# A three-layer block (attention, state-space, two routed feed-forwards): softplus as one ScalarE function, router maxima as an exponential's bias, the last residual sum on TensorE, and a new placement

## The reference

```
x = x + attention(LN(x))      # RMS norm, 16 heads of 16, causal; returns xn + out
x = x + ffn(LN(x))
x = x + ssm(LN(x))
x = x + ffn(LN(x))

ffn(x):  base = x W + b;  shared = low-rank of rank 16
         gate = softmax(x Wr + br) over 6 experts, the two largest kept and renormalised
         routed = sum over experts of weight * (x A_e) B_e, rank 16
ssm(x):  xc = silu(causal conv of 4 taps);  delta = softplus(xc Wd + bd);  B = xc Wb;  C = xc Wc
         h[t] = exp(A * delta[t]) * h[t-1] + delta[t] * xc[t] * B[t]     (256 features x 16 states)
         y[t] = sum over states of h[t] * C[t]
         return (y * sigmoid(x Wg + bg)) Wo + bo
```

## Time and profile before

| | us |
|---|---|
| median of 3 runs | 2177.48 (2174.78 to 2177.67) |
| the profiled execution, device time | 2174.6 |
| its span, first to last instruction | 2172.8 |

### The profile page before, as it was taken

One profiled execution on the slowest core, in us unless ns is written; L12 is line 12 of the kernel. 1 busy time (PEld: TensorE's weight loads), 2 busy tenths in 40 slices (PEclk: granted clock), 3 DMA queues, 4 the chain that ended last, 5 costly groups with the idle time before them and its releaser, 6 DMA issues.

```text
span 2172.8 us, 33597 instructions
## 1 busy us (share of the span) xinstructions
PE 1840.5 (85%) x11393; PEld 1129.0 (52%) x11424; DVE 1675.5 (77%) x2570; ACT 1407.8 (65%) x2724; POOL 1087.5 (50%) x946
## 2 busy tenths in 40 slices
PE   5779788988889898988989888998989898868765
PEld 3446454646556464646556464655556464535333
DVE  5343678889788888879787888879887888977673
ACT  2445767686676767686775867687775777664531
POOL 0000365555455464656465454656555564666672
PEclk8999999999999999999999999999999999989887
DMA  4312377666767576666767576667767577651110
GB/s 114 83 53 58 92 156 152 150 138 142 144 149 159 128 168 146 154 136 146 164 133 154 136 157 137 149 138 157 161 136 155 124 161 145 132 113 45 41 57 10
DMA packets 185916, 275.53 MB, mean 127 GB/s; under 512 B 33537, under 2 KB 125586, under 8 KB 185746
## 3 DMA queue, kind: packets, MB, share of 16 engines
q1 hardware_dynamic: 155506, 163.27, 30.4%
q0 software_dynamic: 30240, 110.11, 27.3%
HBM read 128.58 MB, written 34.08 MB: 75 GB/s over the span
## 4 chain that ended last, share of the span: by engine, by line
PE 42%; ACT 19%; DMA 16%; SPq 7%; issue 5%; DVE 5%; POOL 5%; POOLq 0%; ACTq 0%; DVEq 0%
PE bank L312 7%; DMA sk<-qk_parts 6%; PE bank L516 5%; SPq L712 5%; PE bank L321 4%; ACT dec L896 3%; PE bank L370 3%; PE bank L393 3%; ACT pt L781 3%; PE bank L418 3%; DMA out<-X 3%; PE bank L499 3%; DMA qk_parts<-parts 3%; PE bank L480 2%; DMA y<-hc 2%
## 5 line engine op out<-in xcount | busy, mean ns | idle before, releaser
L1133 DVE TENSOR_TENSOR_SCAN hc<-dec,inp 128x1024 f32<-128x1024 f32 x256 | 613.2, 2395 | 42.5 <-ACT dec L896 30.5
L1304 POOL TENSOR_TENSOR inp<-u,b_all 128x512 f32<-128x512 f32 x256 | 355.3, 1388 | 393.7 <-DVE hc L1133 140.1
L781 ACT ACTIVATE pt<-bank 128x512 f32<-128x512 f32 x640 | 373.8, 597 | 223.8 <-PE bank L395 221.0
L1306 POOL TENSOR_TENSOR inp<-u,b_all 128x512 f32<-128x512 f32 x256 | 375.6, 1467 | 20.1
L370 PE MATMUL bank<-sk,sq 96*128 96x512 bf16 (+3 forms) x1024 | 278.5, 311 | 100.8 <-DMA sk<-qk_parts 64.9
L896 ACT ACTIVATE dec<-dt,a_neg 128x511 f32<-128x511 f32 x512 | 338.0, 717 | 32.6 <-DVE hc L1133 32.6
L1140 DVE TENSOR_TENSOR hc<-hc,bank 128x1024 f32<-128x1024 f32 x242 | 293.9, 1214 | 56.2 <-PE bank L555 55.3
L1313 POOL DMA_DIRECT2D y<-hc x210 | 186.1, 886 | 245.5 <-DMA y<-hc 121.5
L393 PE MATMUL bank<-sq,sk 98*128 98x512 bf16 (+3 forms) x1024 | 274.7, 307 | 35.7 <-ACT pt L781 30.0
L1012 DVE TENSOR_REDUCE mall<-bank 128x1 f32<-128x512 f32 x256 | 172.7, 675 | 108.2 <-PE bank L372 108.0
L370 PEld LDWEIGHTS bank<-sk,sq 96*128 96x128 bf16 x1024 | 102.0, 100 | 219.5 <-DMA sk<-qk_parts 74.0
(11 more groups left out here) (165 smaller groups left out, 3509.9 us busy)
## 6 DMA issues: line engine op xcount, KB each, us to landing
y<-hc POOLq DMA_DIRECT2D x210, 512.0 KB, 5.5
b_all<-b_kept SPq DMA_DIRECT2D x256, 256.0 KB, 4.0
qk_parts<-parts SPq DMA_DIRECT2D x96, 256.0 KB, 2.5
sq<-qk_parts SPq DMA_DIRECT2D x384, 64.0 KB, 3.7
sk<-qk_parts SPq DMA_DIRECT2D x384, 64.0 KB, 3.9
X<-in_x SPq DMA_DIRECT2D x16, 512.0 KB, 6.2
out<-X SPq DMA_DIRECT2D x16, 512.0 KB, 5.8
sq<-hlt SPq DMA_DIRECT2D x256, 2.0 KB
```

The lines of the kernel that those rows point to most:

```text
L781: A(pt[:, n % PT, :], score_bank[unit % 2][:, :], ACT.Exp).then_inc(exp_done.sem, 1)
L1133: V.tensor_tensor_scan(h, d, v, 0.0, ALU.mult, ALU.add).then_inc(scan_done.sem, 1)
L1304: G.tensor_tensor(inp[:, n % 2, 0, :], u[:, 0, :], b_all[:, k % 3, :], ALU.mult).then_inc(pool_own.sem, 1)
L1306: G.tensor_tensor(inp[:, n % 2, 1, :], u[:, 1, :], b_all[:, k % 3, :], ALU.mult).then_inc(inp_ready.sem, 1)
```

## The change

- `dt` comes from ACT's own Softplus, straight from the projection's bank; Relu, Abs, Exp, Ln and DVE's sum are gone. `dt` now has two buffers, and the silu's Tanh is kept in one of them instead of in `sp_t`. Both halves are placed in slot 150 on ACT; on PE they stay in 149 and 152, and both stay in bank `MA`.
- The router's maximum is taken negated and used as the bias of the exponential, one ACT instruction for each of four token blocks; DVE's subtraction is gone.
- In the last feed-forward PE adds X itself, with one more matmul by the identity per token block, and ACT copies the bank to X (`finished`); DVE's `add_to_x` is gone.
- The tables are new. Besides shifts by one to five slots, `load_x` moves from slot -119 to -116, that is from just behind `store` to behind the last third of `stack`. In `BANK` change: res (0, 1) to (0, 0), xn (1, 0) to (0, 0), hw0 1 to 0, up0 (0, 1) to (1, 0), turn1 (0, 1) to (1, 0), up1 (1, 0) to (0, 1).

```diff
     FRAME = 2 * UN * NG
-    PE_AT = {"res": (-32, -31), "xn": (-75, -71), "qk00": (-52, -50, -48), "qk01": (-50, -47, -44), "v": (-26, -32),
-             "qk10": (-6, -4, -3), "qk11": (-4, -2, 0), "ao": (92, 92), "x1": (95, 97), "turn0": (105, 108),
-             "low0": 109, "hw0": 121, "up0": (124, 125), "xs": (135, 135), "conv": (137, 141), "gate": (146, 140),
-             "bc": (149, 152, 154), "dt": (149, 152), "x3": (251, 252), "turn1": (262, 265), "low1": 265, "hw1": 275,
-             "up1": (278, 279)}
...
-    ACT_AT = {"res": (-30, -28), "square_f": 98, "square_s": 127, "square_l": 252, "norm_q": -94, "norm_f": 103,
-              "exp0": 115, "norm_s": 131, "softplus": 153, "decays": 160, "norm_l": 257, "exp1": 266,
-              "xn": (-76, -71), "qk00": (-52, -50, -47), "qk01": (-50, -49, -44), "v": (-26, -32),
-              "qk10": (-6, -4, -1), "qk11": (-4, -2, 0), "ao": (91, 92), "turn0": (104, 108), "low0": 110,
-              "hw0": 120, "xs": (135, 138), "conv": (139, 141), "gate": (146, 140), "bc": (149, 152, 154),
-              "dt": (149, 152), "turn1": (263, 263), "low1": 264, "hw1": 275}
-    DVE_AT = {"add_x1": (94, 96), "in0": 113, "out0": 116, "add_up0": (123, 124), "silu": 144, "delta": 155,
-              "gated": 246, "add_x3": (251, 251), "in1": 265, "out1": 268, "add_up1": (277, 280), "stats_q": -102}
-    POOL_AT = {"rsqrt_f": 99, "rsqrt_s": 124, "rsqrt_q": -104, "inputs": 151, "rsqrt_l": 254, "low": (111, 266)}
-    SP_AT = {"parts": (-43, -4), "load_x": -119, "store_b": 155, "store": 281}
+    PE_AT = {"res": (-32, -30), "xn": (-77, -71), "qk00": (-52, -50, -47), "qk01": (-49, -47, -44), "v": (-26, -32),
+             "qk10": (-7, -4, -3), "qk11": (-4, -2, 0), "ao": (91, 92), "x1": (95, 99), "turn0": (105, 108),
+             "low0": 109, "hw0": 121, "up0": (123, 124), "xs": (135, 135), "conv": (137, 140), "gate": (146, 139),
+             "bc": (149, 152, 154), "dt": (149, 152), "x3": (251, 251), "turn1": (264, 265), "low1": 265, "hw1": 276,
+             "up1": (278, 278)}
...
+    ACT_AT = {"res": (-32, -30), "square_f": 98, "square_s": 124, "square_l": 252, "norm_q": -92, "norm_f": 103,
+              "exp0": 116, "norm_s": 132, "decays": 160, "norm_l": 256, "exp1": 264, "xn": (-78, -72),
+              "qk00": (-52, -50, -46), "qk01": (-49, -49, -44), "v": (-26, -32), "qk10": (-7, -4, -1),
+              "qk11": (-4, -2, 0), "ao": (91, 91), "turn0": (104, 108), "low0": 110, "hw0": 120, "xs": (135, 138),
+              "conv": (139, 140), "gate": (146, 139), "bc": (149, 152, 154), "dt": (150, 150), "turn1": (263, 263),
+              "low1": 264, "hw1": 276, "up1": (278, 279)}
+    DVE_AT = {"add_x1": (94, 96), "in0": 114, "out0": 116, "add_up0": (123, 124), "silu": 143, "delta": 152,
+              "gated": 246, "add_x3": (251, 251), "in1": 265, "out1": 268, "stats_q": -106}
+    POOL_AT = {"rsqrt_f": 98, "rsqrt_s": 121, "rsqrt_q": -103, "inputs": 154, "rsqrt_l": 251, "low": (111, 266)}
+    SP_AT = {"parts": (-42, -4), "load_x": -116, "store_b": 152, "store": 281}
     FINISH = 14
...
                     pe.wait_ge(side["hw", f].free, side["hw", f].at("hw", b, f))
+                if f:
+                    pe.wait_ge(side["x3", j].free, side["x3", j].at("x3", b, j))
                 pe.wait_ge(m.free, m.fill(("up", b, f, j)))
...
                         mm(dst, xt[:, c, tb * P:(tb + 1) * P], wbase[:, c, :], start=(c == 0), stop=False)
+                    if f:
+                        mm(dst, ident[:, :], X[:, b % XS, tb, :], start=False, stop=False)
                     last = mm(dst, hwt[:, tb * P:(tb + 1) * P], wup[:, :], start=False, stop=True)
...
             def exp_logits(b, f):
-                act.wait_ge(lg_done[f].sem, lg_done[f].at(b))
-                A(ex[:, :, :], lg[:, :, :], ACT.Exp).then_inc(ex_done[f].sem, 1)
+                act.wait_ge(top_done[f].sem, top_done[f].at(b))
+                for tb in range(TB):
+                    last = A(ex[:, tb, :], low[:, f, tb, LR - E:], ACT.Exp, bias=top[:, f, tb:tb + 1])
+                last.then_inc(ex_done[f].sem, 1)
...
+            def finished(l, j):
+
+                m = side["up", 1, j]
+                act.wait_ge(m.full, m.at("up", l, 1, j))
+                copy(X[:, l % XS, 2 * j:2 * j + 2, :], m.tile[:, :].rearrange("p (t d) -> p t d", t=2)).then_inc(m.free, 1)
+
             def sigmoid_gate(f, c):
...
                 m = side["conv", c]
+                act.wait_ge(u_done.sem, u_done.at(f - 1))
+                act.wait_ge(dec_ready.sem, dec_ready.at(f - 2))
                 act.wait_ge(m.full, m.at("conv", f, c))
-                A(sp_t[:, c, :], m.tile[:, :], ACT.Tanh, bias=cb[:, c:c + 1])
+                A(dt[:, f % 2, c, :], m.tile[:, :], ACT.Tanh, bias=cb[:, c:c + 1])
                 A(xc[:, c, :], m.tile[:, :], ACT.Identity, bias=cb[:, c:c + 1]).then_inc(m.free, 1)
...
                 act.wait_ge(m.full, m.at("dt", f, g))
-                A(xs_t[:, g, TAPS - 1:], m.tile[:, :], ACT.Relu, bias=bd_c[:, g:g + 1])
-                A(sp_t[:, g, :], m.tile[:, :], ACT.Abs, bias=bd_c[:, g:g + 1]).then_inc(m.free, 1)
-
-            def softplus(f):
-                for g in range(C):
-                    act.wait_ge(side["dt", g].free, side["dt", g].at("dt", f, g))
-                A(sp_t[:, :, :], sp_t[:, :, :], ACT.Exp, scale=-1.0).then_inc(act_own.sem, 1)
-                act.wait_ge(act_own.sem, act_own.one())
-                A(sp_t[:, :, :], sp_t[:, :, :], ACT.Ln, bias=1.0).then_inc(sp_done.sem, 1)
+                A(dt[:, f % 2, g, :], m.tile[:, :], ACT.Softplus, bias=bd_c[:, g:g + 1]).then_inc(m.free, 1)
...
                 if n == 0:
-                    act.wait_ge(dt_done.sem, dt_done.at(s))
+                    for g in range(C):
+                        act.wait_ge(side["dt", g].free, side["dt", g].at("dt", s, g))
                 act.wait_ge(scan_done.sem, scan_done.at(s, n - 1))
                 for c in range(C):
-                    last = A(dec[:, n % 2, c, 1:T], dt[:, c, 1:T], ACT.Exp, scale=a_neg[:, c, n:n + 1])
+                    last = A(dec[:, n % 2, c, 1:T], dt[:, s % 2, c, 1:T], ACT.Exp, scale=a_neg[:, c, n:n + 1])
                 last.then_inc(dec_ready.sem, 1)
...
                     copy_weighted(a, 1)
+                for j in range(2):
+                    if (a := due(now, ACT_AT["up1"][j])) >= 0:
+                        finished(a, j)
                 for j in range(2):
...
                     normalise(a, KIND_S, X[:, a % XS, :, :], tok_f)
-                if (a := due(now, ACT_AT["softplus"])) >= 0:
-                    softplus(a)
                 if (a := due(now, ACT_AT["decays"])) >= 0:
...
-            def add_to_x(b, m, name, j):
-                rows = X[:, b % XS, 2 * j:2 * j + 2, :]
-                dve.wait_ge(m.full, m.at(*name))
-                V.tensor_tensor(rows, m.tile[:, :].rearrange("p (t d) -> p t d", t=2), rows,
-                                ALU.add).then_inc(m.free, 1)
-
             def add_and_sum(b, m, name, j, kind):
...
                 dve.wait_ge(m.free, m.at("low", b, f))
-                V.tensor_reduce(red[:, 0, :], logits, AXX, ALU.max).then_inc(dve_own.sem, 1)
-                dve.wait_ge(dve_own.sem, dve_own.one())
-                V.tensor_tensor(lg[:, :, :], logits, red[:, 0, :, None].to_broadcast([P, TB, E]),
-                                ALU.subtract).then_inc(lg_done[f].sem, 1)
+                V.tensor_reduce(top[:, f, :], logits, AXX, ALU.max, negate=True).then_inc(top_done[f].sem, 1)
...
                     dve.wait_ge(side["conv", c].free, side["conv", c].at("conv", f, c))
-                V.scalar_tensor_tensor(xc[:, :, :], sp_t[:, :, :], 1.0, xc[:, :, :], ALU.add,
+                V.scalar_tensor_tensor(xc[:, :, :], dt[:, f % 2, :, :], 1.0, xc[:, :, :], ALU.add,
                                        ALU.mult).then_inc(xc_done.sem, 1)
...
                 if f:
-                    dve.wait_ge(dec_ready.sem, dec_ready.at(f - 1))
                     dve.wait_ge(inp_ready.sem, inp_ready.at(f - 1))
-                dve.wait_ge(sp_done.sem, sp_done.at(f))
-                V.tensor_tensor(dt[:, :, :], xs_t[:, :, TAPS - 1:], sp_t[:, :, :], ALU.add).then_inc(dt_done.sem, 1)
-                dve.wait_ge(dt_done.sem, dt_done.at(f))
-                V.tensor_tensor(u[:, :, :], dt[:, :, :], xc[:, :, :], ALU.mult).then_inc(u_done.sem, 1)
+                for g in range(C):
+                    dve.wait_ge(side["dt", g].free, side["dt", g].at("dt", f, g))
+                V.tensor_tensor(u[:, :, :], dt[:, f % 2, :, :], xc[:, :, :], ALU.mult).then_inc(u_done.sem, 1)
...
                     router_out(a, 1)
-                for j in range(2):
-                    if (a := due(now, DVE_AT["add_up1"][j])) >= 0:
-                        add_to_x(a, side["up", 1, j], ("up", a, 1, j), j)
                 for j in range(2):
```

(28 more changed lines are left out.)

## The result

| | before | after |
|---|---|---|
| median, us (10 runs each, same chip) | 2175.49 (2168.31 to 2185.18) | 2194.92 (2184.72 to 2209.25) |
| span of the profiled execution | 2172.8 | 2196.9 |
| mean granted clock of PE | 0.952 | 0.937 |
| PE busy / idle in the span | 1840.5 / 332.3 | 1889.0 / 307.9 |

A forecast was written before the change was run, and what follows sets the result against it. The frame was taken as bound by PE and ACT in turns; terms -22.7 - 6.4 + 26.4 - 11 - 4 + 2 = -15.7 gave 2162 us on the median (forecast 2150 to 2173), range 2140 to 2188.

The forecast's parts named there:

- the drain: End of the run, last sequence: u comes about 6 us sooner, the scan then waits for decays; -4 us, bounds 0 and -6.
- the residual: Last feed-forward: four more PE matmuls a sequence, 1.71 us, charged whole in fourteen sequences; +26.4 us in all.
- the other shifts: Remaining slot shifts and bank swaps: order unchanged on SP and POOL, PE's work covers the later exponential; 0 us.
- Load of x behind the stack: SP's queue: PE's eleven sk waits behind the store vanish, -22.7 us, and the low clock after three, -6.4.
- The rival that PE's added work is hidden: PE's busy time is partly slack, so the residual's 23.9 us cost nothing: 2138 us; chance 0.07.
- dt by Softplus: Slot 150: ACT saves 3.3 us a frame, stands 1.98 for the shared bank; PE saves 0.9 in 12 frames, -11 us.
- the slower rival: PE's 1.6 us lost at slot 154 are not regained: +19 instead of -11 us, giving 2192; chance 0.20.
- The clock: Low PE clock (0.75 over 8.6 us) after long waits; only its removal behind three waits was counted, -6.4 us.
- `square_s`: Moved up three slots, ahead of an exponential; covered by 3.8 us on PE, so 0; if short, about 1 us a frame.
- The router: ACT's four exponentials for one add 0.68 us each, 32 times, mostly where ACT waits for PE; +2 us.
- DVE, 0: DVE loses some 3.7 us of work a frame, but PE's waits depend on it less: 0 us, at best -19.

The follow-up runs named there:

- the ladder: Runs between the kernel before and the changed kernel, each adding one group of edits; ratios to the kernel before 0.9887, 1.0018, 0.9918, 0.9988, 1.0088.
- e9: Kernel before with only load_x at slot -116 and the router's maxima as bias of the exponentials: ratio 0.9887.
- e12: Changed kernel with norm_l back at 257 and the dt stretch as before (Relu, Abs, Exp, Ln, DVE's sum, qk10 at -6): ratio 0.9918.
- e10: Kernel before with dt by Softplus, both halves in ACT slot 150, and the first third of q10 and k10 at slot -7: ratio 1.0216.
- e1: Changed kernel with only norm_l put back from slot 256 to 257: ratio 0.9988 to the kernel before, median 2174.80 us.
- the last rung: Step from norm_l at 257 to 256, which completes the changed kernel: ratio 0.9988 to 1.0088, +21.8 us.
- e5: Changed kernel with norm_l at 257 and the middle cast of B and C, with PE's subtraction, in slot 150 instead of 152: ratio 1.0150.
- e13: Kernel before with load_x at -116, the router's bias, dt by Softplus and the first third of q10 and k10 at -7: ratio 1.0129.
- e15: Changed kernel with norm_l at 257, the dt stretch as before and the last residual sum again on DVE: ratio 0.9803, median 2133.35 us.

## Why the prediction was wrong, point by point

The forecast was -15.7 and the steps of the ladder add to +19.1, which is 34.8 apart. Softplus with the drain accounts for 30.2 of it (-15 forecast, +15.2 measured), the load with the router for 2.5, the residual for 2.1, and the other shifts, taken together, for nothing.

- **Load of x behind the stack, -29.1.** Right. It is -31 alone and -22 in the changed kernel, and with the router -24.6, where the prediction has -27.1.
- **The residual, +26.4.** Right in size: +28.5 and 25, and only 9 in the kernel before. The rival that PE's added work is hidden has these runs against it. The Trainium skill's "Perfetto Trace Analysis", section "Identifying the Most-Contended Engine", judges TensorE's headroom by MFU (arithmetic done as a share of the peak) and by its weight-load share, and not by matmul busy time. Here that share is 52% before and 53% after, and 64 added matmuls still cost 28.5 us on top of e9 and 25 in e12.
- **dt by Softplus, -11.** The step that failed. The mechanism was written down correctly: a shared bank, ACT's stand of 2 us, casts and decays behind it, and 1.6 lost at slot 154 (measured 1.93). The sentence that failed is that PE "regains it because no Ln and no load stand before the cast of q". ACT does begin that cast no later, 30.8 us into the frame and 31.0 before; but PE gets back only the 0.97 less 0.31 and the 1.58 that it waited there before, and those do not make up for what it lost. It is 0.54 behind where 0.5 ahead was forecast, and the waits for sk, from which another 0.4 was to come off, grew in e10 (84.8 in all for 64.9). In e1, more frames than in e12 then meet the late exponential at 70 us. This is the mechanism of the slower rival, which put +19 on it with a chance of 0.20; the ladder has +15.2 with what the end gives back, and 20.6 in the frames. It was also taken too lightly that the price hangs on the order in slot 153: with the order of before it is 3.5%.
- **The other shifts, 0.** Right only as a sum, and by luck, since two terms of 21.8 cancel; in its parts this is the second step that failed. `norm_l` was not looked at, and it costs 21.8, by the stand of 4.99 for nm and what follows it. The mechanism that the prediction priced at 1 us a frame for `square_s`, an exponential caught behind an early piece of ACT's work, is what happened, at another piece. The remaining shifts and bank swaps bring 21.8. The kernel before has the wait of 0.99 at L488 (11.9 in 12), which pointed at part of it. That the total comes near the rival's 2192 is partly this luck.
- **The clock.** The prediction charged low clock only where it removed waits of over 3.5 us. It needed the same question for each wait that it might add: in the last rung 27.9 of 31.6 us are busy time for the same matmuls, and in e5 nearly all of the loss.
- **The router, +2, and the drain, -4.** The router brought 7 us alone or nothing beside `load_x` (0.9887 against 0.9856); its size is small. The drain is right for the last sequence: from the start of its convolution to the end 156.2 before and 151.5 after, and 154.9 in e12 to 151.6 in e1. The 7 us that the frame ahead of it also saves were not in the sum.
- **DVE, 0.** Nothing here prices DVE's lost 3.7 us a frame by itself. PE's waits for maxima, over the three lines that wait for them, are 35.3 before and 31.7 after: the largest rose from 19.4 to 28.2, the next fell from 12.7 to 3.2.

That Softplus with its slots costs, that `norm_l` costs and that the residual costs is shown by runs. That the shared bank is why Softplus costs is read from the waits of the traces; no run gave its two halves different banks. That the bank waits at L488 and L501 are part of the gain of the other shifts is read from traces, not tried by itself. Why Softplus is 15 us in the changed kernel and 53 over e9 stays open. In the traces of e10 and e13 waits for sk are larger by 20 us than without it (84.8 against 64.9, 61.6 against 40.2), which is less than half of it. Those two runs also leave `delta`, `inputs` and `store_b` at their old slots, which the changed kernel moves; that was not tried apart.

## What to carry to other kernels

When an edit makes one engine's work shorter but puts its two halves behind each other on one bank, cost it by when the last instruction behind the stand ends, and follow PE through all its waits there, not by the busy time saved. When a table of slots is changed in thirty places, look at each place that moves ahead of an exponential or a cast that the full engine needs: one slot of `norm_l` cost about as much as moving the load had brought. And try a placement together with the form of computation that it was made for: the same form of dt was 1.9% dearer in the other's order.

## What the runs showed of the hardware

What a wait costs could not be read from its length alone. In the changed kernel a wait of 2.97 and mostly one of 0.6 some 3.8 us on went with a granted clock of 0.60 to 0.89 over 16 us, so part of that stretch at 1.2 GHz; in e1 one of 2.72 at the same place, with no second one for an exponential behind it, went with 0.89 in nearly all frames, and one of 1.34 with 1.00. Over a whole run a single slot moved PE's idle time by 3.7 us and its busy time by 27.9, for the same instructions. The mean clock of a run is no measure of its speed either: e15, the fastest, has 0.948 in the profiled execution, and the kernel before 0.952.

Softplus took 687 ns for 128x512 and one table load of 1283 ns each way, the same number and length of loads as Exp and Ln needed before (16 and 15 in the middle of the run). Since both forms have the loads, their number is not what made it dear.
